# Windowed attention in 32 x 64 blocks, with the outputs of a step in two halves around the first projection

## Chip, cores and metric

One core of a Trainium2 chip runs the whole program. The metric is the device time of one execution in microseconds. The five engines each run their own instruction list in order: TensorE (PE, with its weight loads shown apart as PEld), VectorE (DVE), ScalarE (ACT), GpSimd (POOL) and SyncE (SP), which here only issues DMAs. They meet through semaphores alone.

## What is computed

Eight sequences of 512 tokens, 128 features. First a layer of full attention in which only the diagonal weight is used, with a layer norm; then a stack of six layers, each of windowed attention and a feed forward; then a last layer norm. The stack takes nearly all the time:

```python
def local_attention(q, k, v):                 # w = WINDOW = 32
    bq, bk, bv = (t.reshape(b, h, nw, w, d) for t in (q, k, v))
    bk2, bv2 = look(bk), look(bv)             # a window and the one before it: 64 keys
    mask = (it < jb) | (it > jb + w) | (jb == -1)
    sim = jnp.einsum('bhwie,bhwje->bhwij', bq, bk2) * QK_SCALE
    attn = jax.nn.softmax(jnp.where(mask, -big, sim), -1)
    return jnp.einsum('bhwij,bhwje->bhwie', attn, bv2)

for i in range(DEPTH):                        # 6
    x = attn_layer(shift_tokens(x), Wqkv[i], q_scale[i], k_scale[i], Wo[i]) + x
    x = ffn_layer(shift_tokens(x), ln_g[i], ln_b[i], W1[i], b1[i], W2[i], b2[i]) + x
```

Sixteen heads of 64; queries and keys are normalised, scaled and rotated before `local_attention`. So each window of 32 queries sees 64 keys.

## The kernel before

`first_attention` does the first layer. `all_layers` (L737) does the stack: 48 iterations `n` (6 layers x 8 sequences) of 8 steps `p`, 384 steps. A step ("pair", L612) handles four heads (group `g`) of half a sequence (256 tokens), so it has 16 head-and-128-token pieces. The work on one pair is spread over later steps by lags (L606): the transposes of queries and keys come 2 steps after the projection, logits and exponentials 4, the probability transposes 6, outputs and output projection 7. Each engine's order in a step is written out by hand in its own `cycle` (PE L1148, ACT L1452, POOL L1581, DVE L1795); no scheduler moves anything. A wait stops all that follows on its engine.

What one step does, with the lines of the profile:

- **PE.** `project` (L1019 to L1021) makes queries and keys of 128 tokens in three 512-column matmuls, twice a step (`mm` 0 and 1), into banks 0 and 1. `values` (L1031 to L1033) makes values in six 256-column matmuls into bank 2. `transpose_qk` (L1057) turns the rotated queries and keys, four transposes for each `mm`, in banks 5 (`p_ta`) and 6 (`p_tb`). `logits` (L1111 to L1129) first writes the masks as eight bf16 matmuls (L1118) and adds 16 float32 matmuls on top (L1125), each 64 queries by 96 keys of one head, so a row of the softmax has 96 scores of which 64 can be seen. They run on the four 64 x 64 quadrants of the array. `transpose_probs` (L1082) turns the normalised probabilities, four transposes for each of two head pairs `hp`. `outputs` (L1103) multiplies with the values: 16 matmuls, alternately 96 keys (from `V_even`) and 128 keys (`V_odd`), 64 columns of weights and 64 moved, on the two 64-column halves of the array, all into bank 2. `output_projection` (L1143) adds four matmuls into bank 7. A float32 matmul appears in the trace as two instructions, each with its weight load.
- **ACT.** Copies out of PSUM (`probs` L1402, `outputs` L1409, `queries_and_keys` L1424, `values` L1432), squares for the norms (L1417), and the exponentials, eight a step (L1441).
- **DVE.** The row maxima of the logits (L1714), the rotation (`cosines` L1727, `sines` L1737, `add` L1745), sums of squares (L1757), `clamp` L1765, reciprocals L1772.
- **POOL.** The power -1/2 of the norms (L1554), the division of the exponentials (L1564), the scaling of the rotated queries and keys (L1577).
- **SP.** Two DMAs a step (L795, L797) copy the values of `V_odd` to `V_even`, shifted by 32 tokens.

Some steps of an iteration also carry the feed forward of the sequence two iterations earlier, named by the constants of L609: norm (1), transposes (2), the first gate (3), two gates (4), gelu and the down projection of the iteration before (5), two value products (6), the last product and the next sequence's transposes with the low part of x on DVE (7). Their matmuls borrow banks 5 and 6. `end` in each engine drains the pipeline in an order of its own.

The lines of PE's order in a step:

```python
project(n, p, 0)
transpose_probs(n, p, 1)
outputs(pair_at(n, p, LAG_O), n * NP + p)
logits(s, p_s)
transpose_qk(n, p, 0)
project(n, p, 1)
values(n, p)
transpose_qk(n, p, 1)
output_projection(pair_at(n, p, LAG_Y))
transpose_probs(n, p, 0)
```

## Time and profile before

| | us |
|---|---|
| median of 3 runs (lowest, highest) | 3644.83 (3644.83, 3644.84) |
| span of the profiled execution, first to last instruction | 3639.9 |
| eight steps of one iteration (from 2002.29) | 65.39 |
| step 0 of it, which has no feed forward work | 6.92 |
| step 5, with gelu and the down projection | 9.88 |
| first projection of the stack starts at | 445.0 |

The profile gives each instruction's start and duration. Matmuls are pipelined: one instruction's modelled duration (243 ns for a logit matmul) is longer than the distance to the next start, so what a block of matmuls costs is read from start to start. The granted clock of TensorE was 1.00 in all windows read.

### The profile page before, as it was taken

What the parts mean: (1) busy time and instruction counts of PE and PEld (TensorE: products, weight loads), DVE (VectorE), ACT (ScalarE), POOL (GpSimd) and SP (SyncE); (2) the same over time, 40 slices, a digit from 0 to 9 for tenths busy, and PEclk for the clock granted to TensorE, in tenths of its full rate; (3) what the DMA queues carried; (4) which work ended last, traced back from release to release, by engine and by line L of the source; (5) the groups of instructions that cost most, each with busy time, mean ns of one, the idle gap of its engine ahead of it and who ended that gap; (6) DMA issues with size and microseconds to landing.
All of it is one profiled execution on the core that took longest, in us unless ns stands there. A gap on an engine that the chain in (4) does not pass through costs nothing.

```text
span 3639.9 us, 133048 instructions
## 1 busy us (share of the span) xinstructions
PE 3554.4 (98%) x47348; PEld 3028.6 (83%) x47348; DVE 3128.2 (86%) x7021; ACT 3359.9 (92%) x10928; POOL 2732.9 (75%) x2058
## 2 busy tenths in 40 slices
PE   8999999999999999999999999999999999999998
PEld 5666678888888888888888888888888888888887
DVE  8999988888888788887888888889888888888887
ACT  8999889999999999999999999999999999999996
POOL 0111288888888788788888888888888888888884
PEclk9999999999999999999999999999999999999999
DMA  2000011111111111111111111111111111111111
GB/s 102 7 14 10 14 38 43 35 32 34 44 43 41 28 36 36 39 46 36 33 33 40 40 45 35 33 30 43 47 35 37 30 33 45 34 35 36 42 36 39
DMA packets 165015, 132.71 MB, mean 36 GB/s; under 512 B 113933, under 2 KB 124813, under 8 KB 164109
## 3 DMA queue, kind: packets, MB, share of 16 engines
q1 hardware_dynamic: 164365, 124.19, 13.9%
q8 instruction: 390, 6.39, 0.8%
q14 instruction: 260, 2.13, 0.2%
HBM read 25.84 MB, written 4.19 MB: 8 GB/s over the span
## 4 chain that ended last, share of the span: by engine, by line
PE 75%; ACT 5%; DVE 4%; issue 3%; POOL 1%; ACTq 0%; POOLq 0%; DVEq 0%
PE bank L1103 10%; PE bank L1057 10%; PE bank L1082 8%; PE bank L1143 8%; PE bank L1125 6%; PE bank L1019 4%; PE bank L1020 4%; PE bank L1021 4%; PE bank L980 4%; PE bank L1118 3%; PE bank L953 2%; ACT late L1441 2%; PE bank L955 2%; PE bank L954 2%; PE bank L1033 2%
## 5 line engine op out<-in xcount | busy, mean ns | idle before, releaser
L1554 POOL TENSOR_TENSOR a_rn<-a_ssqc,a_minus_half 128x16 f32<-128x16 f32 x384 | 1113.2, 2899 | 490.3 <-DVE a_ssqc L1765 480.6
L1441 ACT ACTIVATE late<-bank,a_negmax 128x96 f32<-128x96 f32 x3072 | 1013.5, 363 | 11.8 <-DVE a_negmax L1714 10.7
L1577 POOL TENSOR_TENSOR a_r<-a_u,a_rn 128x512 f32<-128x512 f32 x768 | 788.3, 1046 | 0.6
L1564 POOL TENSOR_TENSOR a_PN<-late,a_erec 128x384 f32<-128x384 f32 x768 | 730.6, 971 | 9.1 <-PE bank L1082 8.2
L1441 ACT ACTIVATION_READ_ACCUMULATOR late<-bank,a_negmax 128x1 f32 x3072 | 708.7, 231 | 0.0
L1424 ACT ACTIVATE a_QK<-bank 128x512 f32<-128x512 f32 x768 | 467.8, 609 | 122.5 <-PE bank L1057 122.5
L1737 DVE TENSOR_TENSOR a_v<-bank,a_rot_s 128x512 f32<-128x512 f32 x768 | 523.1, 681 | 0.0
L1727 DVE TENSOR_TENSOR a_u<-bank,a_rot_c 128x512 f32<-128x512 f32 x768 | 521.4, 679 | 1.2 <-ACT a_sq L1417 1.1
L1417 ACT ACTIVATE a_sq<-bank 128x512 f32<-128x512 f32 x768 | 482.7, 628 | 42.2 <-PE bank L1021 12.9
L1402 ACT ACTIVATE late<-bank 128x512 f32<-128x512 f32 x758 | 479.6, 633 | 15.3 <-PE bank L1082 11.4
L1745 DVE TENSOR_TENSOR a_u<-a_u,a_v 128x1024 f32<-128x1024 f32 x384 | 489.5, 1275 | 0.7 <-issue 0.3
L1057 PE MATMUL bank<-ident,a_r 128*128 128x128 f32 x3072 | 482.4, 280 | 3.5 <-DVE a_xl L1646 2.3
L1757 DVE TENSOR_REDUCE a_ssq<-a_sq 128x16 f32<-128x1024 f32 x384 | 463.9, 1208 | 17.4 <-issue 16.7
L1082 PE MATMUL bank<-ident,a_PN 128*128 128x128 f32 x3072 | 461.2, 273 | 9.1 <-DVE X L1672 7.5
L1082 PEld LDWEIGHTS bank<-ident,a_PN 128*128 128x128 f32 x3072 | 367.2, 141 | 75.3 <-issue 30.0
L1714 DVE TENSOR_REDUCE a_negmax<-bank 128x8 f32<-128x768 f32 x384 | 365.1, 951 | 64.7 <-PE bank L1125 64.7
L1143 PE MATMUL bank<-w_out,late 128*128 128x128 f32 x3072 | 406.0, 275 | 0.0
L1103 PE MATMUL bank<-late,a_V_even 96*64 96x64 f32 x6144 | 397.6, 227 | 4.9 <-DVE late L1871 2.8
L1057 PEld LDWEIGHTS bank<-ident,a_r 128*128 128x128 f32 x3072 | 341.2, 141 | 64.8 <-issue 3.9
L1103 PE MATMUL bank<-late,a_V_odd 128*64 128x64 f32 x6144 | 379.1, 221 | 0.0
L1143 PEld LDWEIGHTS bank<-w_out,late 128*128 128x128 f32 x3072 | 373.4, 192 | 0.7 <-ACT late L1409 0.4
L1103 PEld LDWEIGHTS bank<-late,a_V_even 96*64 96x64 f32 x6144 | 310.3, 137 | 70.1 <-ACT late L1402 34.3
(191 smaller groups left out, 8129.7 us busy)
## 6 DMA issues: line engine op xcount, KB each, us to landing
a_V_even<-a_V_odd SPq DMA_DIRECT2D x384, 128.0 KB, 2.3
a_V_even<-a_V_odd SPq DMA_DIRECT2D x192, 64.0 KB, 2.2
late<-in_qkv SPq DMA_DIRECT2D x20, 384.0 KB, 3.8
a_x_sh<-X SPq DMA_DIRECT2D x48, 128.0 KB
a_V_even<-a_V_odd SPq DMA_DIRECT2D x192, 32.0 KB, 1.9
a_x_sh<-X SPq DMA_DIRECT2D x48, 127.0 KB
late<-X SPq DMA_DIRECT2D x47, 128.0 KB
late<-X SPq DMA_DIRECT2D x47, 127.0 KB
```

The source lines that it names most:

```text
L1057: ins = pe.transpose(p_t[mm][:, c * P:(c + 1) * P], r[:, t.par, mm * 512 + c * P:mm * 512 + (c + 1) * P], ident[:, :])
L1082: ins = pe.transpose(p_t[hp][:, i * P:(i + 1) * P], PN[:, t.par, 2 * hp + i // 2, first:first + P], ident[:, :])
L1103: ins = pe.matmul(p_vo[q, hp * CQ + i * 64:hp * CQ + (i + 1) * 64], V[:, c:c + DH], PT[keys, o.par, 4 * hp + i, side:side + 64], start=Tru ...
L1143: ins = pe.matmul(p_y[:, i * P:(i + 1) * P], OT[:, y.par, hp, mm * P:(mm + 1) * P], w.out[:, 2 * y.g + hp, :], start=(y.pos + hp == 0 and ...
L1417: act.activation(sq[:, mm * 512:(mm + 1) * 512], p_qk[mm][:, :], ACT.Square).then_inc(S[f"sq{mm}"], 1)
L1441: ins = act.activation(E[:, s.par, k, :], scores[:, i % 2, col:col + KW], ACT.Exp, bias=negmax[:, s.par, k:k + 1], accum_out=esum[:, s.par ...
L1554: pool.tensor_tensor(rn[:, a.par, :], ssqc[:, a.par, :], minus_half[:, :], ALU.pow).then_inc(S["rn"], 1)
L1564: pool.tensor_tensor(PN[:, s.par, 2 * hp:2 * hp + 2, :].rearrange("p i (b k) -> p i b k", b=2)[:, :, :, 0:KW], spread(E[:, s.par, half, :] ...
L1577: pool.tensor_tensor(heads(r[:, a.par, half]), heads(u[:, a.par, half]), rn[:, a.par, mm * 2 * HG:(mm + 1) * 2 * HG].unsqueeze(2).to_broad ...
L1727: dve.tensor_tensor(view(u[:, a.par, mm * 512:(mm + 1) * 512]), view(p_qk[mm][:, :]), tab, ALU.mult).then_inc(S["u_rot"], 1)
L1737: dve.tensor_tensor(halves(v[:, mm * 512:(mm + 1) * 512]), halves(p_qk[mm][:, :])[:, :, :, ::-1, :], tab, ALU.mult).then_inc(S[f"v_rot{mm} ...
L1745: dve.tensor_tensor(u[:, a.par, :], u[:, a.par, :], v[:, :], ALU.add).then_inc(S["u"], 1)
```

## The change

The attention is cut in blocks of 32 queries by 64 keys, `KW` from 96 to 64. Index `c` (0 to 3) stands for a 128-token tile of the pair and, in each 64-token half of it (`half`), the first or the second 32 queries: for the second (`own` 1) the 64 keys are that half of the tile itself (`V_nat`), for the first (`own` 0) they lie 32 tokens earlier (`V_sh`, of which the first DMA now copies 96 rows instead of 64). The logits of `c` go to the 32 partitions `32 c`, with the scores of the two heads of a pair in two banks and eight blocks of 64 columns side by side; the probabilities of a step fill four 128 x 128 tiles instead of eight of 96 used columns, so four transposes turn them and one ACT copy brings them back. The outputs become 32 matmuls of 64 keys, 64 columns of weights, 32 moved columns, into two banks (5 and 6, `p_vo` and `p_tb`), in two halves by `hp`: one ahead of the first projection, one behind it. One ACT copy reads both banks. Exponentials are eight of 64 columns.

The order in a step and the lags are new: the first part of the key and query transposes (`mm` 0) now comes last in PE's step and with lag 1, the logits stand behind the values, the exponentials and maxima have lag 5, rotation of `mm` 1, sums and powers are one step later on DVE and POOL. Waits go with it: the outputs wait for `qk_out1` (their second bank is that of the key transposes), the transposes of `mm` 1 and the feed forward matmuls in `p_tb` wait for `o_out`. `values` still waits for `o_out` of the pair whose outputs use its bank, which are now made in the same step, just ahead.

```diff
-KW = 3 * WIN
+KW = 2 * WIN
-LAG_T, LAG_S, LAG_PT, LAG_O, LAG_Y = 2, 4, 6, 7, 7
+LAG_R, LAG_T0, LAG_T1, LAG_Q0, LAG_Q1, LAG_L, LAG_S, LAG_PT, LAG_O, LAG_Y = 1, 1, 2, 2, 3, 4, 5, 6, 7, 7
-                sp.dma_start(V_even[WIN:KW, a.g, m:m + 2, :], V_odd[0:64, a.g, m:m + 2, :]).then_inc(S[name], 16)
+                sp.dma_start(V_sh[WIN:P, a.g, m:m + 2, :], V_nat[0:P - WIN, a.g, m:m + 2, :]).then_inc(S[name], 16)
...
-            def prob_transposes(t, hp):
-                for i in range(4):
-                    first = KW if i % 2 else 0
-                    ins = pe.transpose(p_t[hp][:, i * P:(i + 1) * P], PN[:, t.par, 2 * hp + i // 2, first:first + P], ident[:, :])
+            def prob_transposes(t):
+                for k in range(4):
+                    ins = pe.transpose(p_ta[:, k * P:(k + 1) * P], PN[:, t.par, k, :], ident[:, :])
...
-                    for hp in range(2):
-                        for i in range(4):
-                            keys = slice(0, P if i % 2 else KW)
-                            V = (V_odd if i % 2 else V_even)[keys, o.g, 2 * o.half + i // 2, :]
+                    pe.wait_ge(S["qk_out1"], keys_out)
...
+                if o:
+                    for c in range(4):
+                        m, own = divmod(c, 2)
+                        V, col = V_nat if own else V_sh, hp * P + c * WIN
+                        for half in range(2):
+                            keys = slice(KW * half, KW * half + KW)
                             for e in range(2):
-                                q, c, side = slice(64 * e, 64 * e + 64), hp * P + 64 * e, 64 * ((e + i) % 2)
-                                ins = pe.matmul(p_vo[q, hp * CQ + i * 64:hp * CQ + (i + 1) * 64], V[:, c:c + DH],
-                                                PT[keys, o.par, 4 * hp + i, side:side + 64], start=True, stop=True)
+                                q, v = slice(64 * e, 64 * e + 64), hp * P + 64 * e
+                                ins = pe.matmul(p_o[half][q, col:col + WIN], V[keys, o.g, 2 * o.half + m, v:v + DH],
+                                                PT[keys, o.par, 2 * e + hp, c * WIN:(c + 1) * WIN], start=True, stop=True,
+                                                skip_group_check=True)
...
+                    for c in range(4):
+                        for e in range(2):
+                            rows = slice(WIN * c, WIN * c + WIN)
+                            pe.matmul(scores[rows, e, :], ident_b[sides[e], 64 * e:64 * e + WIN],
+                                      masks[sides[e], int(s.half > 0 or c > 0), :], start=True, stop=True, skip_group_check=True)
                     for hp in range(2):
-                        for i in range(4):
-                            first, col = 64 * (4 * s.half + i), (2 * hp + i // 2) * KW
-                            for e in range(2):
+                        for half in range(2):
+                            col = (2 * hp + half) * KW
+                            for c in range(4):
+                                first = (2 * s.half + c // 2) * P + half * KW + c % 2 * WIN
+                                for e in range(2):
+                                    ins = pe.matmul(scores[WIN * c:WIN * c + WIN, e, col:col + KW],
+                                                    QK[sides[e], s.gpar, hp, WIN + first:WIN + first + WIN],
+                                                    QK[sides[e], s.gpar, 2 + hp, first:first + KW], start=False, stop=True,
+                                                    skip_group_check=True)
```

PE's and ACT's order in a step after (feed forward parts left out; the waits of DVE and POOL follow the lags):

```python
# PE
outputs(o, 0, *moved); project(n, p, 0); outputs(o, 1, *moved); project(n, p, 1); values(n, p)
logits(s, p_s); transpose_probs(n, p); transpose_qk(n, p, 1); output_projection(...); transpose_qk(n, p, 0)
# ACT
queries_and_keys(pair_at(n, p, LAG_Q1), 1); exps(s, 0, 0, p_s); exps(s, 0, 1, p_s); queries_and_keys(pair_at(n, p, LAG_Q0), 0)
exps(s, 1, 0, p_s); outputs(pair_at(n, p, LAG_O)); exps(s, 1, 1, p_s)
squares(n, p, 0); squares(n, p, 1); values(n, p); probs(pair_at(n, p, LAG_PT))
```

The feed forward matmuls move with the banks: the ones in `p_ta` stand before or behind the second projection, the ones in `p_tb`, the transposes of the next x and the down projection stand between the values and the logits. On DVE the low part of x (`low_x`) now follows `cosines` and `sines` of `mm` 0.

## Rows read from the trace of the kernel before

**Rows 1.** The page, parts 1 and 4: busy time of the engines, and the last chain.
```profile
PE 3554.4 (98%) x47348; PEld 3028.6 (83%) x47348; DVE 3128.2 (86%) x7021; ACT 3359.9 (92%) x10928; POOL 2732.9 (75%) x2058
...
PE 75%; ACT 5%; DVE 4%; issue 3%; POOL 1%; ACTq 0%; POOLq 0%; DVEq 0%
```

**Rows 2.** Busy time by window (steps 0, 1, 5, 6 of one iteration, sum of eight).
```profile
2002.29:2009.21 6.92, 6.92 (x110) 6.25 (x109) 6.92 (x15) 6.24 (x23) 5.19 (x4) 1.00 0.17 40
2009.21:2016.32 7.11, 7.01 (x112) 6.27 (x110) 7.03 (x21) 6.75 (x25) 7.00 (x7) 1.00 0.15 35
...
2040.58:2050.46 9.88, 9.84 (x134) 8.97 (x134) 7.14 (x13) 9.33 (x35) 8.62 (x6) 1.00 0.14 31
2050.46:2059.63 9.17, 8.77 (x116) 7.35 (x115) 5.35 (x8) 8.47 (x19) 5.95 (x5) 1.00 0.09 24
...
sum 65.39, PE 64.07 PEld 56.03 DVE 56.91 ACT 61.30 POOL 54.86; mean PE 8.01 PEld 7.00 DVE 7.11 ACT 7.66 POOL 6.86
```

**Rows 3.** Timeline of the matmuls of one plain step: start us, us, what.
```profile
2002.29 0.47 PE L1019 MATMUL bank<-a_wh,a_xh 128*128 128x512 f32 x1
...
2003.07 0.60 PE L1082 MATMUL bank<-ident,a_PN 128*128 128x128 f32 x4
2003.59 0.34 PE L1103 MATMUL bank<-late,a_V_even 96*64 96x64 f32 x4
...
2004.34 0.29 PE L1103 MATMUL bank<-late,a_V_even 96*64 96x64 f32 x4
2004.46 0.29 PE L1103 MATMUL bank<-late,a_V_odd 128*64 128x64 f32 x4
2004.68 0.36 PE L1118 MATMUL bank<-a_masks,a_ident_b 64*64 64x192 bf16 x8
2004.87 0.83 PE L1125 MATMUL bank<-a_QK 64*64 64x96 f32 x32
2005.63 0.66 PE L1057 MATMUL bank<-ident,a_r 128*128 128x128 f32 x4
2006.04 0.48 PE L1019 MATMUL bank<-a_wh,a_xh 128*128 128x512 f32 x1
...
2006.82 0.28 PE L1031 MATMUL bank<-a_wh,a_xh 128*128 128x256 f32 x1
...
2007.52 0.60 PE L1057 MATMUL bank<-ident,a_r 128*128 128x128 f32 x4
2007.96 1.06 PE L1143 MATMUL bank<-w_out,late 128*128 128x128 f32 x8
2008.85 0.60 PE L1082 MATMUL bank<-ident,a_PN 128*128 128x128 f32 x4
2009.21 0.48 PE L1019 MATMUL bank<-a_wh,a_xh 128*128 128x512 f32 x1
```

**Rows 4.** The mask weight loads of that step (timeline, weight loads of PE).
```profile
2004.67 0.14 PEld L1118 LDWEIGHTS bank<-a_masks,a_ident_b 64*64 64x64 bf16 x8
```

**Rows 5.** Groups of instructions by line and shape: busy us, mean ns.
```profile
L1441 ACT ACTIVATE late<-bank,a_negmax 128x96 f32<-128x96 f32 x3072 | 1013.5, 363 | 11.8 <-DVE a_negmax L1714 10.7
...
L1564 POOL TENSOR_TENSOR a_PN<-late,a_erec 128x384 f32<-128x384 f32 x768 | 730.6, 971 | 9.1 <-PE bank L1082 8.2 <-DVE a_erec L1772 0.8
...
L1714 DVE TENSOR_REDUCE a_negmax<-bank 128x8 f32<-128x768 f32 x384 | 365.1, 951 | 64.7 <-PE bank L1125 64.7
...
L1125 PE MATMUL bank<-a_QK 64*64 64x96 f32 x12288 | 318.8, 243 | 0.0
...
L1006 PE MATMUL bank<-w_cols,w_w 128*128 128x1 f32 x48 | 5.7, 240 | 0.0
```

**Rows 6.** Timeline: a copy on ACT and the weight load that waited for it.
```profile
2009.81 0.63 ACT L1402 ACTIVATE late<-bank 128x512 f32<-128x512 f32 x1
...
2010.52 0.20 PEld L1103 LDWEIGHTS bank<-late,a_V_even 96*64 96x64 f32 x4 [0.17 <-ACT late L1402]
```

**Rows 7.** The page, part 6: the widest of the value moves.
```profile
a_V_even<-a_V_odd SPq DMA_DIRECT2D x384, 128.0 KB, 2.3
```

434 lines of the change are left out of this document (206 added, 228 removed).

## The prediction, before the result was known

> **What bounds the kernel now.** I read the page's shares first. PE is busy 98% of the span, ACT 92%, DVE 86%, and the last chain is 75% PE [rows 1]. A busy PE counts the modelled tails of its matmuls, so I then cut one iteration of eight steps into windows [rows 2]. The eight steps sum to 65.39 us. A plain step (step 0) lasts 6.92 us with PE busy for all of it and ACT for 6.24; step 1 is 7.11. Step 5 carries the down projection and gelu (9.88), step 6 two up projections and the first product (9.17, PE busy 8.77). Third, the matmul timeline of step 0 [rows 3] has no hole from one first projection (2002.29) to the next (2009.21): blocks of work follow each other at 0.78, 0.52, 1.09, 0.19, 0.76, 0.41, 0.78, 0.70, 0.44, 0.89 and 0.36 us, which is 6.92. So PE's instruction stream sets a plain step, ACT is a close second, and the change has to be priced in PE starts, block by block. There are 384 steps: 0.01 us of PE time in each is 3.8 us of the total.
>
> **The change, part by part.** Unless said otherwise, per step.
>
> *Probability transposes.* The blocks of a step now need four transposes, not eight. Four in a row cost 0.44 us (2007.52 to 2007.96) [rows 3]. PE -0.44.
>
> *Logits.* Before, 16 float32 matmuls, 32 instructions, cover 64 queries by 96 keys on four quadrants. They start within 0.83 - 0.24 = 0.59 us (one instruction lasts 243 ns [rows 5]); as eight rounds of four that is seven gaps of 0.084, 0.66 in all, and the block of 0.76 holds 0.10 more until the next transposes start [rows 3]. After, 32 matmuls, 64 instructions, cover 32 by 64 on eight tiles (64 rows by 32 columns). If eight tiles run side by side as four do now, it is again eight rounds, of 64 moved columns instead of 96. A round of the outputs, which move 64 float32 columns, takes 0.117 / 2 = 0.058 (2004.34 to 2004.46, four instructions on two tiles) [rows 3]. So 0.47 for 0.66: PE -0.19. Bounds: eight rounds scaled by columns (0.44) below; four tiles at a time (16 rounds, 0.93) above. I take the first, since the mask weights, eight loads of 104 ns each in a stretch of 0.14 [rows 4], show that tiles load side by side and start a few ns apart. The masks go from 192 to 256 columns, one set of eight instead of two of four: about nothing.
>
> *Outputs.* Before, 16 matmuls (32 instructions) on two column tiles: 16 rounds at 0.058, 0.93. After, 32 matmuls (64 instructions) on four quadrants: again 16 rounds, with 32 moved columns but still 64 columns of weights. Which of the two sets a round? With one moved column, 48 float32 loads of 128 columns are busy 5.7 us, 0.119 each [rows 5], so 64 columns of weights cost 0.059: the load holds the round at 0.058 whatever is moved. PE 0. Bounds: 0.029 a round if the moved columns set it (-0.47), and 0.084, the only round in the trace that loads four 64-column float32 weights (+0.42). I stay at 0.058 because the 96 moved columns explain the 0.084.
>
> *Switches between array shapes.* A block of transposes that is followed by a block on smaller tiles takes 0.52 instead of 0.44 (2003.07 to 2003.59), and the logits end with 0.10 over their rounds [rows 3]: some 0.09 a change of shape. Before, a step has three (into the outputs, from them to masks and logits, back). After, it has six: into and out of each half of the outputs, into and out of the logits. PE +3 x 0.09 = +0.27. Nearest zero would be a drain hidden behind the 512-column projections; the highest row is 0.10.
>
> *The added wait.* The values write the bank in which half of the outputs lies, and now come only one projection after it; before, logits, transposes and a projection lay between. Last output to copy on ACT to values: the last output matmul takes 0.24, the copy 0.63, and the weight load that waited for such a copy began 0.08 after its end (2010.44 to 2010.52) [rows 6], in sum 0.95-1.0. The cover is one switch and one projection, 0.15 + 0.78. So +0.05 if ACT is free; it has three exponentials' worth of room before that copy. Behind this wait stand the values, logits, all transposes and the output projection, so a late ACT would cost PE directly. The outputs also wait for the second key copy (ACT's first work in the step, done about 0.5 us before by my walk), at nothing.
>
> *Feeding PE.* 120 more PE records a step (60 loads, 60 matmuls), 144 of them in masks and logits in a row. The logits row shows 32 instructions with their loads in 0.76; nothing shows whether twice that is fed in half the time. I add 0.05.
>
> *Other engines.* ACT: eight exponentials of 64 columns for 96 (363 ns each now, mostly fixed [rows 5]), 0.2 less, and one 512-column copy less, 0.6. DVE: the maximum reads 512 values for 768 (951 ns), 0.3 less. POOL: two products of 256 for 384 (971 ns each), 0.5 less. None bounds a plain step, so all this counts 0; what it buys is room for the waits. The value moves carry 96 rows for 64, land in 2.3 us [rows 7] and have over six steps: 0. Larger lags add one step's tail of DVE and POOL work at the end: +2 us once.
>
> *Sum.* -0.44 - 0.19 + 0 + 0.27 + 0.05 + 0.05 = -0.26 in a plain step. The eight steps hold 65.39 - 8 x 6.92 = 10.0 us beside their plain work, mostly feed forward matmuls. I expect their stalls to stay in sum: in step 7 the low part of the next x now comes behind two rotations on DVE and the second key transposes wait for it (+0.3 an iteration), in step 6 (9.17, PE busy 8.77 [rows 2]) ACT's lighter work gives as much back. So -0.26 x 384 = -100, and with the tail -98. The profiled execution has a span of 3639.9 and the runs a median of 3644.8, 4.9 above; both shift alike, to a span near 3542 and **3547 us**.
>
> A rule against this sum: the Trainium skill ("TensorE: Matmul & The Clock Gate", "Wait — 56ns, not 53.3ns?") says that starts of matmuls never come closer than about 25 ns, however small they are. By it, as an estimate from that page, the 128 output and logit instructions of a step would need 3.2 us where I put 1.4, and the total would pass 4200 (rival D is this as rows would have it). This trace doesn't agree where tiles differ: eight mask loads start within 0.04 us [rows 4], and the 32 logit instructions within 0.59, 19 ns apart [rows 3].
>
> **The rivals.**
> *A, the logits run four at a time, or PE is fed too slowly for eight.* 16 rounds of 0.058 add 0.46: +177, so 3724. For it: no row has more than four tiles busy at once, and 144 records come in a row. Against: the side-by-side loads. It decides at 0.26: once the logits' rounds take over 0.73 us in all, the gain is gone. **Slower side.**
> *B, four loads of 64 columns disturb each other in the outputs.* At 0.084 a round +0.42, +160: 3707. It turns at 0.074 a round.
> *C, the new order stalls.* The copy of the outputs sits behind three pairs of exponentials and the gelu of step 5; if values wait 0.2 more in each step (+77), 3624; with 0.26 and more, no gain. Step 6 (PE busy 8.77 of 9.17) shows that ACT does hold PE after the gelu.
> *D, PE has a fixed slot of about 19 ns for an instruction.* Then 128 instructions take 2.4, +1.0 a step: about 3940. The mask loads speak against it.
> *E, better than I think:* switches hidden behind projections, or stalls of the feed forward steps gone with ACT's 0.8 us of room: 0.1 to 0.15 less a step, 3490 to 3510.
>
> **How the numbers follow.** My case 0.46 (3515 to 3580), E 0.10, C 0.18 (3580 to 3670), A 0.15, B 0.07, D 0.04. The range leaves out D, the upper two thirds of A and half of B, 0.18 in all: 3480 to 3700; below it reaches past E towards lighter output rounds. The likeliest case's own is 3515 to 3580. Faster by over 0.2% (7 us, about what a measurement of this kernel tells from none): my case, E and two thirds of C, 0.68. Within 0.2%: 0.05, from C and A. Slower: 0.27, the rest of C, A and B, and D.
>
> **What would show it.** Right: plain steps near 6.6 us with PE without holes; 64 logit instructions starting within about 0.45; output groups of eight instructions every 0.117; half as many probability transposes; values starting 0.9 to 1.0 after the last output of the second half. Wrong: logit starts spread over 0.73 or more (A), output rounds over 0.074 (B), holes in the weight loads ahead of the values or behind a copy on ACT (C), equal gaps of some 19 ns (D).

## The result, and the profile after

The changed kernel takes **3682.55 us** (median of 4 runs, 3681.28 to 3685.77) where the kernel before takes 3644.84: ratio 1.0104, interval 1.0092 to 1.0117. It is 1.0% slower. The forecast was 3547, which is faster than before.

The page of the changed kernel gives the busy time of the engines (before: [rows 1]). ACT, DVE and POOL lost 289, 118 and 239 us of work, near the 0.8, 0.3 and 0.5 us a step of the forecast, and PE is busy for a smaller share of a longer span:

```profile
span 3680.0 us, 177745 instructions
PE 3543.4 (96%) x70388; PEld 2899.5 (79%) x70388; DVE 3009.8 (82%) x7016; ACT 3071.3 (83%) x10549; POOL 2494.2 (68%) x2057
```

Busy time in steps 0 to 3 and 6 and 7 of one iteration, and the sum of its eight (before: [rows 2]; columns: stretch, us, then PE, PEld, DVE, ACT, POOL busy with counts, granted clock of PE, DMA share, GB/s):

```profile
2087.79:2095.63 7.84, 7.32 (x175) 5.88 (x169) 5.41 (x18) 5.17 (x18) 5.16 (x4) 1.00 0.29 87
2095.63:2103.16 7.53, 6.98 (x174) 5.92 (x169) 7.53 (x16) 6.76 (x31) 7.40 (x8) 1.00 0.13 36
2103.16:2110.49 7.33, 7.33 (x179) 6.31 (x173) 6.37 (x12) 6.48 (x26) 6.41 (x6) 1.00 0.16 36
...
2136.25:2145.14 8.89, 8.43 (x181) 6.91 (x175) 7.00 (x13) 7.30 (x33) 6.09 (x6) 1.00 0.12 34
2145.14:2153.40 8.26, 8.24 (x181) 6.77 (x176) 7.38 (x14) 6.75 (x26) 5.93 (x6) 1.00 0.13 30
sum 65.61, PE 64.06 PEld 53.66 DVE 52.40 ACT 55.02 POOL 49.88; mean PE 8.01 PEld 6.71 DVE 6.55 ACT 6.88 POOL 6.24
```

Step 0, which carries no feed-forward matmul, was 6.92 with PE busy throughout and is 7.84 with half a microsecond of PE idle. In step 1 DVE is busy for all of its 7.53 us. Now the waits of PE and of DVE between 500 and 3500 us (in all, times, longest):

```profile
PE bank L1011 <- DVE a_v L1730: 40.3, 53, 3.0
PE bank L1054 <- POOL a_r L1566: 23.6, 44, 2.2
PE bank L952 <- ACT a_QK L1415: 20.6, 46, 1.1
```
```profile
DVE a_st L531 <- DMA late<-X: 106.3, 45, 4.1
```

The DMA wait, once an iteration, did not exist before. Its place in the timeline of DVE (an excerpt around step 0's start at 2087.79):

```profile
2079.82 0.68 DVE L1773 TENSOR_TENSOR X<-X,bank 128x512 f32<-128x512 f32 x1
...
2087.60 0.68 DVE L1730 TENSOR_TENSOR a_v<-bank,a_rot_s 128x512 f32<-128x512 f32 x1
2090.64 0.87 DVE L531 BATCH_NORM_STATS2 a_st<-late 128x6 f32<-128x128 f32 x4 [2.35 <-DMA late<-X]
...
2092.04 1.23 DVE L1737 TENSOR_TENSOR a_u<-a_u,a_v 128x1024 f32<-128x1024 f32 x1
```

and what follows it on POOL, and then on PE:

```profile
2093.35 1.04 POOL L1566 TENSOR_TENSOR a_r<-a_u,a_rn 128x512 f32<-128x512 f32 x1 [2.68 <-DVE a_u L1737]
```
```profile
2094.44 0.66 PE L1054 MATMUL bank<-ident,a_r 128*128 128x128 f32 x4 [0.52 <-POOL a_r L1566]
```

This is the chain. SP issues three loads of the residual sum's result, shifted by a token (L88 to L90, `late<-X`), for the statistics of the feed-forward input. The change put the residual sum of step 7 (L1773) behind DVE's sines and the statistics of step 0 (L531) ahead of the rotation's sum (L1737). The loads are issued from 2080.53 to 2082.06, and DVE's wait for them ends at about 2090.6, 10.1 us after the first. Most of that time is a slow tail: the 16 DMA engines are busy for 0.71 of the window 2081.7 to 2082.5, with 162 GB/s, and for 0.09 of the window 2082.5 to 2088.5, with 21 GB/s. No run shows why the tail is slow. DVE stands still for 2.35 us, and the rotation, POOL's `units` and PE's transposes are queued behind it. Step 1 gets the rest: the second projection waits for the sines.

What else is missing against the forecast lies in PE's own stream. Here is the timeline of the matmuls of a step without holes (step 2, which has the four transposes L947 of the feed forward, 0.41 us, in it; before: [rows 3]):

```profile
2103.73 0.39 PE L1013 MATMUL bank<-a_wl,a_xh 128*128 128x512 f32 x1
2104.05 0.32 PE L1101 MATMUL bank<-late,a_V_sh 64*64 64x32 f32 x8
2104.19 0.30 PE L1101 MATMUL bank<-late,a_V_nat 64*64 64x32 f32 x8
2104.31 0.30 PE L1101 MATMUL bank<-late,a_V_sh 64*64 64x32 f32 x8
2104.42 0.30 PE L1101 MATMUL bank<-late,a_V_nat 64*64 64x32 f32 x8
2104.65 0.65 PE L947 MATMUL bank<-ident,late 128*128 128x128 f32 x4
...
2106.64 0.30 PE L1117 MATMUL bank<-a_masks,a_ident_b 64*32 64x256 bf16 x8
2106.76 0.84 PE L1125 MATMUL bank<-a_QK 64*32 64x64 f32 x64
2107.54 0.66 PE L1078 MATMUL bank<-ident,a_PN 128*128 128x128 f32 x4
2108.03 0.60 PE L1054 MATMUL bank<-ident,a_r 128*128 128x128 f32 x4
```

7.33 less 0.41 is 6.92: what a plain step took before. The output groups of eight come every 0.117 as forecast. But the logits take 0.77 from their first start to the next block, where they took 0.76 [rows 3], and none of the forecast's -0.26 is there.

### The profile page after: what moved, and what is told of

The parts are those of the page before. It is cut to its first block and busy times, and to the rows that moved or that the text cites. A ratio compares the mean times of both kernels' runs of the same rounds, so it can differ in the third digit from the quotient of the medians.

```text
span 3680.0 us, 177745 instructions
## 1 busy us (share of the span) xinstructions
PE 3543.4 (96%) x70388; PEld 2899.5 (79%) x70388; DVE 3009.8 (82%) x7016; ACT 3071.3 (83%) x10549; POOL 2494.2 (68%) x2057
## 5 line engine op out<-in xcount | busy, mean ns | idle before, releaser
L1432 ACT ACTIVATE late<-bank,a_negmax 128x64 f32<-128x64 f32 x3072 | 945.4, 331 | 105.2 <-DVE a_negmax L1709 104.3
L1555 POOL TENSOR_TENSOR a_PN<-late,a_erec 128x256 f32<-128x256 f32 x768 | 487.7, 635 | 355.0 <-DVE a_erec L1762 344.3
L1054 PE MATMUL bank<-ident,a_r 128*128 128x128 f32 x3072 | 466.0, 275 | 28.6 <-POOL a_r L1566 24.5
L1101 PEld LDWEIGHTS bank<-late,a_V_sh 64*64 64x64 f32 x12288 | 325.6, 133 | 211.9 <-issue 209.4
L1737 DVE TENSOR_TENSOR a_u<-a_u,a_v 128x1024 f32<-128x1024 f32 x384 | 470.5, 1225 | 26.0 <-DVE a_v L1730 0.5
L1408 ACT ACTIVATE a_sq<-bank 128x512 f32<-128x512 f32 x768 | 441.8, 621 | 6.9 <-PE bank L1013 6.4
L1101 PE MATMUL bank<-late,a_V_sh 64*64 64x32 f32 x12288 | 424.0, 224 | 8.9 <-ACT a_QK L1415 6.2
L1394 ACT ACTIVATE late<-bank 128x512 f32<-128x512 f32 x379 | 226.3, 597 | 240.3 <-PE bank L1078 240.3
L1011 PE MATMUL bank<-a_wh,a_xh 128*128 128x512 f32 x768 | 367.3, 478 | 49.5 <-DVE a_v L1730 48.9
L1101 PE MATMUL bank<-late,a_V_nat 64*64 64x32 f32 x12288 | 408.9, 219 | 0.0
L1054 PEld LDWEIGHTS bank<-ident,a_r 128*128 128x128 f32 x3072 | 356.9, 142 | 47.9 <-POOL a_r L1566 34.1
L1400 ACT ACTIVATE late<-bank 128x512 f32<-128x512 f32 x384 | 233.5, 608 | 146.0 <-PE bank L1101 145.8
L1101 PEld LDWEIGHTS bank<-late,a_V_nat 64*64 64x64 f32 x12288 | 329.9, 135 | 0.0
```

The lines of the kernel that those rows point to most:

```text
L1054: ins = pe.transpose(p_t[mm][:, c * P:(c + 1) * P], r[:, t.par, mm * 512 + c * P:mm * 512 + (c + 1) * P], ident[:, :])
L1101: ins = pe.matmul(p_o[half][q, col:col + WIN], V[keys, o.g, 2 * o.half + m, v:v + DH], PT[keys, o.par, 2 * e + hp, c * WIN:(c + 1) * WIN], ...
L1432: ins = act.activation(E[:, s.par, k, :], scores[:, hp, col:col + KW], ACT.Exp, bias=negmax[:, s.par, k:k + 1], accum_out=esum[:, s.par, k ...
L1555: pool.tensor_tensor(PN[:, s.par, 2 * hp:2 * hp + 2, :].rearrange("p i (b k) -> p (i b) k", b=2), E[:, s.par, half, :], erec[:, s.par, hal ...
L1737: dve.tensor_tensor(u[:, a.par, :], u[:, a.par, :], v[:, :], ALU.add).then_inc(S["u"], 1)
```

## The experiments

Each run was measured beside runs of the kernel before on the same chip; their medians lie between 3644.7 and 3646.8 us. The last column of the table at the end has the ratios, and a difference of a few microseconds between two changed kernels is clear of noise only where their intervals don't overlap.

**Theory S**: the new order of DVE's queue makes the holes of steps 0 and 1. **Theory T**: the split of the outputs costs PE two more changes of array shape than need be. **Theory F**: the logits are bound by how fast their records reach the array. Rivals: the values' new wait for the copy of the outputs (rival C), the granted clock, and rounds of tiles (each of the eight tiles is busy with one instruction's columns before it takes the next). A step is measured from one first projection matmul to the next, and its length is given as the median over the iterations.

### The statistics moved

```diff
                 sines(b, 1)
...
-                if p == 0:
-                    stats(n)
                 add(b)
...
                 sines(a, 0)
+                if p == 0:
+                    stats(n)
```

> Edit: the changed kernel, with the statistics of the feed-forward input moved in step 0 of each iteration from ahead of the rotation's sum to behind the first half's sines, on VectorE alone. Theory S (stalls of order): in the profile after the change VectorE waits some 2.35 us in step 0 for the shifted loads (45 times, 106.3 us in all), and everything behind the statistics is late by it: the rotated sum, POOL's units, PE's transposes of step 0 (0.65 us a step), and the second projection of step 1 (0.83 us). If the wait's place is the cause, the loads land before the statistics are reached, the wait falls below 20 us in all, steps 0 and 1 lose 1.2 us or more together, the half-speed stretches of PE's clock that followed a hole of 1.6 us go, and the time is 3682.6 - 45 x 1.2 = 3629, or 3615 to 3640. Rival C (the wait of the values or of the copy behind the exponentials, the clock, or PE itself bounds these steps): the wait moves or goes, and the time stays within 8 us of 3682.

Measured 3642.43: 40 us less, just above the stated range. The DMA wait is in no row of DVE's waits any more, and the transposes' wait for POOL is gone, but the other one grew:

```profile
PE bank L1011 <- DVE a_v L1730: 46.8, 50, 3.0
PE bank L952 <- ACT a_QK L1415: 22.5, 48, 1.1
```

Medians over the iterations: step 0 7.83 to 7.10, step 1 7.53 to 7.80. So only the half of step 0 was cured: the statistics now end step 0's queue and push step 1's sines back.

### The residual sum moved instead

```diff
+                if p == P_X:
+                    residual(n)
                 if p == P_GELU + 1:
                     feed_forward_out(n)
                 maxima(s, p_s)
...
-                if p == P_X:
-                    residual(n)
```

> Edit: the changed kernel, with the residual sum of step 7 put first on VectorE again, as the kernel before has it, ahead of the maxima and the feed-forward output; the statistics stay where the change put them. The shifted loads are issued behind this sum. Theory S: the loads were issued at 2080.5 to 2082.1 against a sum that then stood behind the sines; some 1.5 to 2 us of queue work lie ahead of it, so the loads land about 1.7 us earlier, the wait of 2.35 us in step 0 falls to about 0.7, and the time to 3682.6 - 45 x 0.9 = 3642 or so (3630 to 3665), less of a gain than the statistics' move gives. Rival: the sum waits itself for the output projection, nothing lands earlier, and the time stays within 8 us of 3682.

Measured 3655.77, within the stated 3630 to 3665. Rows of DVE's waits:

```profile
DVE X L1773 <- PE bank L1143: 73.9, 44, 1.7
...
DVE a_st L531 <- DMA late<-X: 10.3, 39, 0.4
```

Steps 0 and 1 fall to 7.10 and 7.09, both at once, with the statistics left where the change had put them. So the time at which the loads are issued is what counted; the place of the statistics did not have to change. But the sum now waits for the output projection, and step 7 goes from 8.26 to 9.17. Between the two lies the place of run e5, behind the maxima:

```diff
                 maxima(s, p_s)
+                if p == P_X:
+                    residual(n)
                 norms(b)
```

> Edit: the changed kernel, with the residual sum of step 7 on VectorE between the maxima and the norms (the change has it behind the sines, some 2.3 us of queue work later; first in the step it waited 1.7 us for the output projection, 44 times, in the second run). Theory S: both ends are avoided: the projection has ended by then, so the wait for it falls from 73.9 us in all to under 20; the shifted loads still land in time, so the wait of 106.3 us in step 0 falls to under 30; steps 0 and 1 come to about 7.1 each as in the second run, step 7 stays near 8.3 instead of 9.17, and the time is 3655.8 - 45 x 0.7 = 3624, or 3618 to 3640. Rival: the 2.1 us of the loads are late wherever the sum stands but first, and the time is above 3650.

Measured 3630.77, ratio 0.9962 (0.9950 to 0.9975). This one moved line gives back **52 us**, and with it the change is faster than the kernel before by 0.4%. The rows of DVE:

```profile
DVE X L1773 <- PE bank L1143: 49.6, 45, 1.2
...
DVE a_st L531 <- DMA late<-X: 33.8, 41, 1.0
```

Both waits fell less than expected (under 20 and under 30 were stated), and step 7 stays at 8.58. Steps 0 and 1 are at 7.10 and 7.09, with no hole on PE. The rival of the granted clock can claim a part at most: the profiled executions had 0.993 with the change and 0.996 in e5, which over their spans is some 11 us of full clock, an estimate from these two means. That clock was lost behind PE's holes (last section).

### The two halves of the outputs together

```diff
-                outputs(o, 0, *moved)
                 project(n, p, 0)
+                outputs(o, 0, *moved)
                 outputs(o, 1, *moved)
```

This is run e4; in e3 both stand ahead of `project(n, p, 0)`.

> Edit: the changed kernel, with both halves of the outputs ahead of the first projection, no half behind it. Theory T (switches): each change of array shape costs about 0.09 us in the trace of after (0.149 from the last output to the first projection matmul where matmuls of one shape follow in less), and the move takes away two of six. PE's plain step falls by 0.18 us, and the time by up to 384 x 0.18 = 69 to 3614 if nothing else waits, 3640 if half of it is lost to the holes of steps 0, 1 and 6. Rival (the split hides something: the first projection then starts 0.47 us later, so its squares, the rotation and all behind them do): the steps that already wait get worse and the time stays at 3675 or above.

> Edit: the changed kernel, with both halves of the outputs behind the first projection. Theory T: two switches fewer as well, 0.18 us a step, up to 3614; the first projection starts 0.47 us earlier, which helps the rotation chain, but the output bank is then filled 0.47 later and the values stand closer behind the copy that frees it. If that copy bounds (rival C of the prediction), PE shows a wait of the values for the copy of 0.1 to 0.5 us a step and the time is 3640 to 3680; if not, this is the faster of the two moves by up to 10 us.

Measured 3628.89 and **3620.49**: 54 and 62 us less, near the 69 that theory T had at most. Steps 2 to 5 fall by 0.31 to 0.34 each in e4. The hole of step 0 stayed, with DVE's order untouched, and grew: the step goes from 7.83 to 8.15 in e4 and to 8.12 in e3. Step 1 stayed at 7.53. These two runs don't decide rival C. In e4 the second half of the outputs stands as far from the values as it did, and a wait that is covered by the modelled tail of the matmul before shows in no row of PE's waits. e3, which puts a whole projection more between them, is not faster. What rival C's wait costs is read from e10 and e11 below. Nor are the 8 us between e3 and e4 a price of the place alone: in some iterations of e3 a wait of 1.28 us in step 0 (L1054 for POOL) is followed by a granted clock of 0.57 (window 1545 to 1549), and its five runs had a clock of 0.986 to 0.990 for 0.991 and 0.992 in e4.

Both causes together, e5 and e4:

> Edit: the changed kernel, with both: the residual sum between maxima and norms, and both halves of the outputs behind the first projection. If the causes are separate they add: 3682.6 - 62 (run e4) - 59 (e5 as expected) = 3562, or 3550 to 3590, with plain steps of 7.0 less the turn's 0.42 and steps 0 and 1 near 6.8 to 7.0. Rival: with PE faster by 0.3 us a step another engine's queue sets the steps (ScalarE with 83% of its span busy, VectorE with 82%), and the gain over e4 is under 30 us.

Measured **3559.03**, ratio 0.9764 (0.9751 to 0.9778). The causes add, and a little more: 52 + 62 = 114 by the single runs, 124 measured. The excess fits step 0, where the shorter stream of PE only lengthened the hole in e4 and is a gain here. Step 0 of this kernel:

```profile
2084.64 0.39 PE L1013 MATMUL bank<-a_wl,a_xh 128*128 128x512 f32 x1
2084.96 0.32 PE L1101 MATMUL bank<-late,a_V_sh 64*64 64x32 f32 x8
...
2085.80 0.30 PE L1101 MATMUL bank<-late,a_V_nat 64*64 64x32 f32 x8
2086.02 0.51 PE L1011 MATMUL bank<-a_wh,a_xh 128*128 128x512 f32 x1
2086.37 0.39 PE L1012 MATMUL bank<-a_wh,a_xl 128*128 128x512 f32 x1
2086.60 0.40 PE L1013 MATMUL bank<-a_wl,a_xh 128*128 128x512 f32 x1
2086.91 0.36 PE L1023 MATMUL bank<-a_wh,a_xh 128*128 128x256 f32 x1
```

Here a change of shape can be read from both sides. The outputs begin 0.32 behind the last projection matmul, where two of those follow each other in 0.23. The last output instruction is 0.15 ahead of the next projection. The second matmul of that projection starts 0.35 behind the first, where 0.23 is usual (2086.37 to 2086.60). To put a block of smaller tiles between two projections costs, by medians, 0.321 + 0.149 + 0.343 less 0.235 + 0.233: **0.345 us beside the block's own length**. Step 0 is 7.10 in e5 and 6.77 here, so one pair of changes, into the smaller tiles and out of them, was worth 0.33 of it.

### The logits

This kernel leaves out half of the moved columns, with the same number of instructions: of each block's 64 keys only the first 32 are multiplied.

```diff
-matmul(scores[WIN * c:WIN * c + WIN, e, col:col + KW], ..., QK[sides[e], s.gpar, 2 + hp, first:first + KW], ...
+matmul(scores[WIN * c:WIN * c + WIN, e, col:col + WIN], ..., QK[sides[e], s.gpar, 2 + hp, first:first + WIN], ...
```

> Edit: the changed kernel, whose logits take only the first 32 of the 64 keys of a block (the other 32 scores keep the mask's value, so half of the products of queries and keys are left out); the number of instructions and their loads are unchanged. Theory F (the logits are bound by how fast their records reach the array): behind the first two rounds the starts stay one per 8.4 ns, and the 64 of a step start within 0.60 to 0.65 us as before. Rival R (bound by the tiles: eight in flight, each with its load and its 64 columns, in rounds): half the columns take 13 to 27 ns off a round of 67, so the starts come every 5 to 7 ns and the 64 within 0.50 or less. The forecast had 0.47 for these 64.

```profile
2043.80 0.30 PE L1117 MATMUL bank<-a_masks,a_ident_b 64*32 64x256 bf16 x8
2043.92 0.75 PE L1125 MATMUL bank<-a_QK 64*32 64x32 f32 x64
2044.63 0.63 PE L1078 MATMUL bank<-ident,a_PN 128*128 128x128 f32 x4
```

The block went from 0.773 to 0.678 by medians for half of the columns (0.71 in the step shown). Median starts of the first, 9th, 17th ... of the 64 instructions, in ns from the first, over 384 steps:

```
as changed   0  56 112 187 307 390 457 532   last 626
half keys    0  28  60 187 271 337 404 471   last 554
```

From the 33rd on, half keys come at one per 8.3 ns (two, then 16.7 ns, then two). In the full kernel the same stretch has the same step of about 17 ns for two, though 64 columns move, and 9.4 ns an instruction in all. The first rounds do follow the columns: 56 ns and 28 ns for eight. So neither side of the expectation holds alone, and 0.554 lay outside both of the stated ranges, about midway between them. The burst starts at a pace that the columns set and then runs at one that they hardly change. Each instruction has its weight load, so 8.3 ns an instruction is one record per 4.2 ns.

Run e15 looks at the same question in another way, and prices a pair of shape changes by itself:

```diff
-                logits(s, p_s)
+                logits(s, p_s, (0,))
                 transpose_probs(n, p)
+                logits(s, p_s, (1,))
```

> Edit: as e7, with the logits in two parts, the masks and the first 32 ahead of the transposes of the probabilities and the other 32 behind them: one more pair of switches and nothing else. Theory T2 (a pair costs 0.345 us: 0.321 into the outputs, 0.149 out of them and 0.343 behind the first projection matmul, less 0.235 and 0.233): the plain step is 0.3 longer, 384 x 0.3 = 115, so about 3668, 3640 to 3685. Theory T1 (0.09 a switch, as the forecast had it): 0.18, 3622 or less. Theory F in both: each part of 32 spans about 0.30, as the first 32 of 64 did (0.298), since behind the first rounds they come one per 8.3 ns; by the rounds of eight alone it would be 0.20.

```profile
2045.65 0.30 PE L1119 MATMUL bank<-a_masks,a_ident_b 64*32 64x256 bf16 x8
2045.77 0.53 PE L1133 MATMUL bank<-a_QK 64*32 64x64 f32 x32
2046.23 0.66 PE L1078 MATMUL bank<-ident,a_PN 128*128 128x128 f32 x4
2046.82 0.45 PE L1133 MATMUL bank<-a_QK 64*32 64x64 f32 x32
2047.21 0.66 PE L1054 MATMUL bank<-ident,a_r 128*128 128x128 f32 x4
```

Measured 3600.88, 48 us above e7. By the total that is in T1's range (3622 or less) and outside T2's; only the steps tell the two apart. Step 0 went from 6.77 to 6.99. The first 32, behind the masks, start within 0.314, as stated. The other 32, behind four long transposes, start within **0.238**, which theory F had put at 0.30 too: behind their first eight (80 ns) they come at 56 ns for eight, the pace of the first rounds. The same instructions, with the same tiles, keep that pace when long instructions stand before them and lose it behind the masks. That fits theory F, in which the supply of records is what is short behind the masks and has time to build up behind the transposes. It is argued from the two runs: no row shows the supply itself, and no run takes away the masks, eight 256-column matmuls on the same tiles, which might hold the logits behind them instead.

The two parts together are 0.075 shorter than one of 64, and the rest of the step is 0.30 longer. That is the price of this pair, near T2's 0.345 and far from the forecast's 0.18. The total came out lower than T2's since the 0.075 were not counted and the pair cost next to nothing in steps 1 (0.02), 6 (0.05) and 7 (0.00), which had waits anyway.

### What else was tried on the way down

> Edit: as e6, and in step 6 the first matmuls of the feed-forward's second half (the group that waited 0.48 us a time for ScalarE's copy of queries and keys, 0.81 in e4) stand behind the second projection instead of ahead of it. If that wait only lacked cover, step 6 falls by 0.5 to 0.8 and the time is 20 to 35 us under e6's. Rival: VectorE's product, which waits for these matmuls, is then late by the 0.9 us of the projection and the step keeps its length: within 8 us of e6.

The diff, against e6:

```diff
-                if p == P_VALUES:
-                    up(n, p, 0, 1, p_ta)
                 if p == P_TURN:
                     turn(n)
                 project(n, p, 1)
+                if p == P_VALUES:
+                    up(n, p, 0, 1, p_ta)
```

Measured 3553.26, 5.8 less with intervals that overlap: the rival. The wait of L952 fell from 41.8 to 7.1 us, and step 6 by 0.13 only: the values' wait for ScalarE's copy of the outputs rose from 1.6 to 10.8 us in turn.

> Edit: as e7, and in every step VectorE does the second half's cosines and sines ahead of the norms and the clamp. Theory S: in e7 the second projection still waits for the sines in steps 1 and 7 (0.631 from the last output to it in step 1 where 0.149 is the least, 0.610 for 0.23 in step 7), 46 us in all; the sines come 1.2 us earlier in VectorE's queue, so both waits go: 45 x (0.48 + 0.38) = 39, and the time is 3553.3 - 39 = 3514, or 3508 to 3530. Rival: the norms and the clamp are late by as much, POOL's power and units behind them, and PE's transposes of queries and keys wait instead: within 10 us of e7 or slower.

```diff
-                norms(b)
                 cosines(b, 1)
-                clamp(b)
                 sines(b, 1)
+                norms(b)
+                clamp(b)
```

Measured 3564.97, 11.7 above e7: the rival. The wait for the sines left the list, and POOL's and the input's took its place:

```profile
PE bank L1054 <- DVE a_xl L1641: 30.0, 46, 1.2
PE bank L1054 <- POOL a_r L1566: 22.9, 51, 1.2
```

Step 2 shows it: 7.00 in e7, 7.49 here, and no other step moved by over 0.03.

> Edit: as e5 (outputs split as the change has them), with the rotations first as in e9. It shows what the change gives with VectorE's order cured and nothing else touched: steps 0 and 1 are at 7.095 and 7.094 already; what is left there is at 954 to 1011 in step 7 and in the last three iterations, so 3630.8 less 5 to 15, 3616 to 3626. The forecast's 3547 would need the plain step 0.2 us shorter, which theory T (three more switches, transposes not straight ahead of a projection, logits not faster) excludes.

Measured 3638.29, 7.5 above e5 and not the 5 to 15 below it that were expected; the two intervals just overlap. The medians of all eight steps are within 0.03 of e5's, step 2 too (7.33 and 7.32), so with the split this order is neutral in an ordinary iteration. What it loses lies in the first iteration (53.5 us for 49.1) and in those behind a layer's boundary (66.9 for 65.7).

> Edit: as e9 with both halves of the outputs ahead of the first projection instead of behind it. Theory C (the wait added at the values): the values follow the last output by 1.03 us in steps 0, 1 and 5 whether the outputs are split or not, and PE is held there by 0.155 us (0.307 and 0.194 between starts where 0.228 and 0.118 are usual); with the outputs ahead a whole projection more lies between, so 0.155 x 3 x 48 = 22 us go, less 0.17 a step where the transposes no longer stand straight ahead of a projection (0.203 for 0.029 between starts), 384 x 0.17 = 65: the time is 40 us above e9, 3545 to 3565. Rival (the price of the place is not there, only the switch): within 10 us of e9.

Measured 3556.26: within the stated times by luck, as these were counted from the 3514 expected of e9. Against the measured e9 it is 8.7 faster, not 40 slower, which is the rival. The wait of the values is gone (0.307 and 0.194 between starts became 0.237 and 0.120 in step 0), so that part was right. The 65 us for the lost place of the transposes did not come: what is lost between transposes and outputs (0.203 for 0.029) is won between the projections, which now follow each other directly. So a pair of shape changes costs the same in either place.

> Edit: as e9, and in steps 0, 1 and 5 the transposes of the probabilities stand between the second projection and the values instead of behind the logits. Theory C: they cover the 0.155 us for which the values wait for ScalarE's copy of the outputs, and follow a projection without a switch, while the queries' and keys' transposes then take the switch behind the logits: 0.15 to 0.25 us a step of three, 48 iterations, so 20 to 35 us under e9. Rival: POOL's probabilities aren't there so early and the transposes wait for them: slower than e9.

```diff
+                if p in (0, 1, 5):
+                    transpose_probs(n, p)
                 values(n, p)
...
-                transpose_probs(n, p)
+                if p not in (0, 1, 5):
+                    transpose_probs(n, p)
```

Measured 3552.52, 12.5 under e9, short of the stated 20 to 35. Steps 0 and 5 fall by 0.158 and 0.134, which is the wait; step 1 rises by 0.156, as the transposes of queries and keys come earlier and wait for POOL (37.8 us in all, 22.9 before).

> Edit: as e7 with both halves of the outputs ahead of the first projection (norms first again). From e10 against e9: the wait of the values for the copy goes (0.142 us in step 0), the switches are as many, and 8.7 us were gained. Theory: 3553.3 - 9 = 3544, or 3538 to 3552. Rival: the first projection is 1.06 us later, so the sines that already hold the second projection in steps 1 and 7 hold it longer, and nothing is gained: 3550 to 3565.

> Edit: as e13, and in step 7 the transposes of the next block's input stand ahead of the values instead of behind them (the copy that frees their bank is early enough with the outputs ahead). The queries' and keys' transposes of that step wait 0.47 us for the low part of the input (0.494 between starts where 0.028 or 0.109 is usual); the chain through ScalarE and VectorE starts 0.7 us earlier, so the wait goes: 45 x 0.4 = 18 under e13. Rival: ScalarE takes the high part behind the squares and VectorE the low part behind its sines whenever it comes: within 5 us of e13.

```diff
+                if p == P_X and n + 1 < NI:
+                    transpose_x(n + 1)
                 values(n, p)
...
-                if p == P_X and n + 1 < NI:
-                    transpose_x(n + 1)
```

Measured 3549.36 and 3548.96. The first is 3.9 under e7, where 9 were expected and where the intervals overlap. Its steps show why it gains little: step 0 fell by 0.158 and step 1 rose by 0.150, where the second projection waits for the sines. The second gained nothing (rival): the chain of the input's low part isn't set by PE's place for it.

| run | us | ratio to before, interval |
|---|---|---|
| after (the change) | 3682.55 | 1.0104 (1.0092, 1.0117) |
| e1 statistics later | 3642.43 | 0.9992 (0.9983, 1.0001) |
| e2 residual first | 3655.77 | 1.0030 (1.0018, 1.0041) |
| e3 outputs ahead | 3628.89 | 0.9956 (0.9942, 0.9970) |
| e4 outputs behind | 3620.49 | 0.9932 (0.9919, 0.9944) |
| e5 residual in the middle | 3630.77 | 0.9962 (0.9950, 0.9975) |
| e6 = e4 + e5 | 3559.03 | 0.9764 (0.9751, 0.9778) |
| e7 = e6, up later | 3553.26 | 0.9746 (0.9733, 0.9759) |
| e8 half keys (a single run) | 3659.55 | |
| e9 = e7, rotations first | 3564.97 | 0.9782 (0.9768, 0.9795) |
| e10 = e9, outputs ahead | 3556.26 | 0.9756 (0.9743, 0.9769) |
| e11 = e9, probabilities earlier | 3552.52 | 0.9745 (0.9732, 0.9758) |
| e12 = e5, rotations first | 3638.29 | 0.9980 (0.9971, 0.9989) |
| e13 = e7, outputs ahead | 3549.36 | 0.9734 (0.9719, 0.9748) |
| e14 = e13, x earlier | 3548.96 | 0.9732 (0.9718, 0.9747) |
| e15 = e7, logits split | 3600.88 | 0.9876 (0.9859, 0.9892) |

## Why the prediction was wrong

It was wrong in direction: -98 forecast, +38 measured. That the time still lies inside the range is luck: the room up to 3700 was there for rivals A, B and C, and none of them came at the price it was given. Of the 136 us between forecast and result, 52 are a hole outside PE's stream, shown by e5. The rest is in PE's stream, and there the steps of the sum can be laid beside the trace. Below is step 0 with the hole cured (e5, 7.096) against before (6.923), each part the distance from its first matmul start to that of the next part, medians of 41 iterations:

| part of the step | forecast | measured | |
|---|---|---|---|
| transposes | -0.44 | -0.27 | 1.73 to 1.46 |
| masks and logits, with the feeding of PE | -0.19 + 0.05 | -0.06 | 0.95 to 0.89 |
| shape changes, in the other parts | +0.27 | +0.30 | |
| added wait of the values | +0.05 | +0.155 in steps 0, 1, 5; about 0 in the rest | |
| first to second projection matmul, twice, and the like in the values | 0 | +0.05 | |
| sum | -0.26 | +0.17 | |

*Shape changes.* This is the term that failed most. The forecast had three more at 0.09, +0.27. In the table +0.30 stands against it (outputs +0.11, the start of the outputs behind the projection +0.09, values to masks +0.09), but two other rows hold a part of the same price. A pair of changes around a block costs 0.30 to 0.345 (e6, e15; step 0 of e5 against e6 gives 0.33), since beside the entry, whose 0.09 I had read, there are the exit (0.149) and the slower second projection matmul behind it (+0.11), which I hadn't. The three changes with what they take from the transposes and from the projections (0.30 + 0.17 + 0.05) come to 0.52, one and a half such pairs, for 0.27. Laid over 384 steps the split's own pair is 127 us, of which e4 and e6 got 62 and 72 back: in steps 1, 6 and 7 another wait took its place.

*Transposes.* A block of four does cost 0.44, as the row said [rows 3]. Before, two blocks stood straight ahead of a projection, whose first matmul came 0.03 after the last transpose where another transpose comes after 0.11; the second projection matmul then came 0.32 after the first and not 0.23, so this early start is no gain in sum. After, the outputs or a later place in the step took that neighbour away, and behind the outputs the second projection matmul is late all the same (0.34). That is the 0.17 by which the row falls short. I priced the removed block by a row of its length and didn't ask what its neighbours lose.

*Logits.* Eight tiles do run side by side at the forecast's pace (0.056 a round), for the first two rounds. Then something holds them that the columns hardly change (e8) and that is not there behind long instructions (e15): most likely the supply of records, of which I wrote that nothing showed it and for which I put 0.05. The 64 start within 0.63 for the forecast's 0.47, and their block is 0.01 longer than before and not 0.14 shorter. The -0.06 of the table is the masks alone (0.19 to 0.12), which the forecast had put at about nothing. Rival A named this cause, and priced it at its far end (0.93 where 0.63 came).

*The added wait.* The mechanism was right: the trace of the changed kernel gives 1.00 from the last output (2089.14) to the values' weight load (2090.14), and the size in the three steps with nothing else in between was three times mine. Over eight steps 0.155 x 3 / 8 is 0.058, so the average came out right, with a spread that I hadn't foreseen. By e10 and e11 this wait is worth 0.13 to 0.16 in a step that has it, 22 us in all at most. Rival C, which put the loss here, was wrong in its place; that a new order would stall was right, on DVE.

*Output rounds.* 0.058 held, so rivals B and D fell. (The row that I read for the weight loads is that of the matmuls; the loads of the same line are busy 5.8 us for 5.7, which changes nothing.) The Trainium skill's least distance of 25 ns between starts ("TensorE: Matmul & The Clock Gate", "Wait — 56ns, not 53.3ns?") doesn't hold across tiles in this trace: the first eight logit instructions, on eight tiles, start within 23 ns.

*The stalls "stay in sum".* This sentence failed, and with it the direction. I looked at the waits that the change names and at the low part of x, and moved the statistics and the residual sum without following the DMA between them: from the first issue to the end of the wait the loads take 10.1 us, longer than a step, and before the change the residual sum stood first in step 7 and the statistics late in step 0. The forecast also wrote that no other engine bounds a plain step and that ACT is the close second. Its own rows say otherwise: DVE is busy for 6.92 of 6.92 us in step 0 and 7.03 of 7.11 in step 1 [rows 2]. The 86% of the page is an average over steps with other limits, and in these two steps DVE had no room for a stop of 2.35 us.

The other steps did gain: in e5 steps 2, 4 and 6 are 0.42, 0.45 and 0.35 under before, steps 3 and 5 by 0.1, and step 7 is 0.53 above, where the transposes wait for the low part of the input, about as forecast (0.49 between starts where 0.11 is usual, for +0.3). What the gains of the other steps consist of was not taken apart. It also remains open why DVE can't deliver that low part sooner; e9, e12 and e14 did not bring it forward. That the last three iterations are 1.4 to 3 us longer each than before (69.3, 69.2 and 67.7 in e5 for 66.3) wasn't looked into with a run.

With the two flaws undone the kernel takes 3559 in e6 and 3549 in e13, next to the forecast's 3547. That is no confirmation: without the split there are two shape changes fewer, for which the forecast's own terms would take off another 0.18 x 384 = 69 us, to 3478. The sizes in its sum stay wrong; what was right is that the smaller blocks can be made to pay.

## What to carry to other kernels

Price a change of array shape on both sides of the block, and with what the neighbours lose. Read it where such a block stands between two blocks of one kind, less the distance without it. For each instruction that is moved in an in-order queue, follow what its result starts, DMAs above all, to the place where it is awaited, and compare the time left there with the time from issue to landing. Look for engines without room step by step, not by their share of the whole span. When a many-instruction burst is shortened per instruction, read the pace in the middle of the burst: its start doesn't show it.

## What the runs showed of the hardware that was not expected

- 64 small matmul instructions with a weight load each, behind the 8 of the masks, start at 56 ns for eight at first and at 9.4 ns each later; with half of the columns at 28 ns for eight and 8.3 ns each. Behind four 128-column transposes the second 32 of them keep to 56 ns for eight (e15).
- The clock fell behind short holes. In the first step of a new layer, where DVE also makes the rotation tables (L732, L733), PE stood still for 1.59 us, after another hole of 0.59 some 3 us earlier. The window of 3.6 us that follows was granted 0.54 of the clock, so nearly all of it the half level, 1.2 GHz:

```profile
2030.38 0.77 PE L1011 MATMUL bank<-a_wh,a_xh 128*128 128x512 f32 x1 [1.59 <-DVE a_v L1730]
2030.94 0.63 PE L1012 MATMUL bank<-a_wh,a_xl 128*128 128x512 f32 x1
2031.37 0.63 PE L1013 MATMUL bank<-a_wl,a_xh 128*128 128x512 f32 x1
```
```profile
2027.25:2030.40 3.15, 1.55 (x36) 1.07 (x36) 3.15 (x7) 2.54 (x14) 2.87 (x4) 0.98 0.02 5
2030.40:2034.00 3.60, 3.60 (x65) 3.09 (x69) 3.33 (x9) 2.59 (x8) 3.47 (x3) 0.54 0.00 0
```

The 512-column matmuls start 0.43 apart in place of 0.23. Iterations behind such a boundary took 68.6 to 69.5 us for 65.5; in e5 and e6, where the holes of steps 0 and 1 are gone or smaller, most take 1.0 to 1.2 and 1.5 to 1.7 us more than their neighbours. At all five boundaries between 900 and 3100 us the hole begins before the fall, so the clock followed the holes rather than made them.
- The third of the shifted loads, the smallest with 0.8 KB, occupies SP's queue for 6.5 us, before and after, while the two before it (128 and 127 KB) trickle in; the value moves behind it wait for that.
